# Two-layer graph network on one core: index loads of 64 tiles asked for a body ahead, and four places for the loads of edges

## The reference

```python
h = relu(layernorm(x))                                   # layer 0
m = relu(concat([h[src], edge_attr_64]) @ W_msg.T + b)
m = relu(m @ W_msg2.T + b2)
x = x + concat([h, segment_sum(m, dst) / max(cnt, 1)]) @ W_apply.T + b_apply
h = relu(layernorm(x))                                   # layer 1
alpha = segment_softmax(edge_weight, dst)
agg = normalize(segment_sum(alpha[:, None] * h[src], dst))
comb = normalize(0.5 * (h @ W_self + b_self + agg @ W_nb + b_nb))
x = x + layernorm(comb) * gamma + beta
```

## Time and profile before

| | |
|---|---|
| median of three runs | 10865.57 us |
| the profiled execution | 10872.07 us |
| its span, first to last instruction | 10870.3 us |
| POOL busy | 6155.9 us (57%), 6448 gathers |
| PE busy | 5331.9 us (49%) |
| DVE busy | 3580.0 us (33%) |
| ACT busy | 1136.7 us (10%) |
| DMA engines, mean | 57 GB/s |
| granted TensorE clock, mean | 0.669 of full speed |

### The profile page before, as it was taken

How to read it: one execution, slowest core, us unless ns; L and a number is a source line. 1 busy time by engine, 2 the same in 40 slices (tenths; PEclk the granted TensorE clock), 3 DMA queues, 4 the chain that set the end, 5 groups by cost and what they waited for, 6 DMA issues and landing times.

```text
span 10870.3 us, 94616 instructions
## 1 busy us (share of the span) xinstructions
PE 5331.9 (49%) x26549; PEld 4117.8 (38%) x26549; DVE 3580.0 (33%) x14159; ACT 1136.7 (10%) x2108; POOL 6155.9 (57%) x6486
## 2 busy tenths in 40 slices
PE   4666666666655555566666533332333233233334
PEld 3444444444444344344444423222222222222224
DVE  4333233323222222222222433333333333333336
ACT  2111111111111111111111200000000000000002
POOL 4555555555554444455555466666666666666663
PEclk7777777777777677777777655655555555555556
DMA  4222222222222222222222222221111111111112
GB/s 151 56 57 54 56 56 55 57 58 57 61 67 56 57 57 59 58 55 56 58 56 57 65 57 56 56 55 49 46 46 47 46 46 47 46 46 47 46 47 72
DMA packets 412673, 618.83 MB, mean 57 GB/s; under 512 B 171795, under 2 KB 274175, under 8 KB 411263
## 3 DMA queue, kind: packets, MB, share of 16 engines
q0 software_dynamic: 206336, 422.99, 15.0%
q1 hardware_dynamic: 192624, 183.30, 6.1%
q10 hardware_dynamic: 13200, 6.56, 0.2%
HBM read 576.45 MB, written 35.92 MB: 56 GB/s over the span
## 4 chain that ended last, share of the span: by engine, by line
another core or an unknown queue 49%; PE 25%; issue 12%; DVE 12%; ACT 1%; DVEq 1%; DMA 0%; SPq 0%; POOL 0%; ACTq 0%; POOLq 0%
PE bank L1056 13%; DVE acc L884 7%; PE bank L1118 6%; PE bank L1115 3%; PE bank L1053 2%; DVE onehot L887 1%; DVE work L887 1%; ACT work L581 1%; DVEq L866 1%; DVEq L884 0%; DVE xq L711 0%; DVE acc L711 0%; DVE acc L995 0%; ACT work L587 0%
## 5 line engine op out<-in xcount | busy, mean ns | idle before, releaser
L493 POOL DMA_INDIRECT rows_ring<-p_table,idx x3224 | 3087.5, 958 | 2951.8 <-DMA idx<-in_src_ring 1790.9
L884 DVE TENSOR_TENSOR acc<-acc,bank 128x128 f32 x6448 | 1826.0, 283 | 7192.7 <-remote 5639.5
L493 POOL DMA_INDIRECT rows_ring<-h_table,idx x3224 | 3052.5, 947 | 1635.2 <-issue 1013.2
L887 DVE TENSOR_SCALAR onehot<-iota,dloc,coef 128x128 f32<-128x128 f32 x4840 | 1703.6, 355 | 16.5 <-ACT coef L558 13.3
L1056 PE MATMUL bank<-work,rows_ring 128*128 128x128 f32 x3216 | 694.6, 370 | 1867.6 <-DVE work L887 665.6
L1056 PE MATMUL bank<-onehot,work 128*128 128x128 f32 x6448 | 1094.4, 325 | 863.4 <-issue 676.4
L1056 PE MATMUL bank<-onehot,rows_ring 128*128 128x128 f32 x3232 | 743.8, 401 | 1247.1 <-remote 594.9
L1056 PEld LDWEIGHTS bank<-work,rows_ring 128*128 128x128 f32 x3216 | 597.9, 270 | 1968.7 <-issue 1911.4
L1056 PEld LDWEIGHTS bank<-onehot,work 128*128 128x128 f32 x6448 | 1002.8, 237 | 898.9 <-issue 711.3
L1056 PEld LDWEIGHTS bank<-onehot,rows_ring 128*128 128x128 f32 x3232 | 651.6, 297 | 1323.7 <-issue 1261.4
L1118 PE MATMUL bank<-work,we_sb 64*128 64x512 f32 x1612 | 1045.4, 724 | 164.7 <-issue 164.1
(11 more groups left out here) (121 smaller groups left out, 1066.1 us busy)
## 6 DMA issues: line engine op xcount, KB each, us to landing
work<-in_edge_t SPq DMA_DIRECT2D x403, 256.0 KB
rows_ring<-p_table,idx POOLq DMA_INDIRECT x3224
rows_ring<-h_table,idx POOLq DMA_INDIRECT x3224
idx<-in_src_ring SPq DMA_DIRECT2D x404, 8.0 KB
ht_rows<-rows_ring SPq DMA_DIRECT2D x25, 256.0 KB, 2.3
p_table<-rows_ring SPq DMA_DIRECT2D x25, 256.0 KB, 2.5
work<-ht_rows SPq DMA_DIRECT2D x25, 256.0 KB
h_table<-work ACTq DMA_DIRECT2D x25, 256.0 KB
```

The lines of the kernel that those rows point to most:

```text
L493: pool.indirect_dma_start(out=rows_ring[:, 16 * h + G * k + j, :], out_offset=None, in_=table[:, :], in_offset=bass.IndirectOffsetOnAxis(a ...
L884: dve.tensor_tensor(win, win, ps_sum[layer][k % slots][:, j * P:(j + 1) * P], ALU.add).then_inc(added, 1)
L887: ins = dve.tensor_scalar(hot_slots[layer][k % slots][:, j * P:(j + 1) * P], iota[:, :], dloc[:, ds(t, 1)], coef[:, ds(t, 1)], ALU.is_equa ...
```

## The change

1. `idx` holds the numbers of 2 x 64 tiles' numbers where it held 2 x 16. One load brings the indices of a pair of bodies (32 KB for 8 KB; 51 loads for a layer instead of 202). Pair p + 1 is asked for in body i = 2p (even, from 2), behind that body's edge loads and behind a wait until PE has done the groups before body i (`m1t_in_psum` or `sums1_in_psum` at 8i). It is first used in body i + 2. POOL waits for indices once in two bodies.
2. `ef_ring` has four places: chunks n = 0, 1 (mod 4) on partitions 0 to 63, 2 and 3 on partitions 64 to 127 of the same columns. `we_sb` is loaded twice, once for each half of the partitions. Chunk n waits for chunk n - 4. Each place has its own semaphore.
3. In a body of layer 0 SP issues four edge chunks, then the indices (even bodies), then `load_pre`, which stood between the halves. In layer 1's tail the loads of `self_rows` stand behind the last index loads.

```diff
-        idx = sb("idx", [P, 2, 4 * G], I32)
+        idx = sb("idx", [P, 2, 16 * G], I32)
-        we_sb = sb("we_sb", [DE, P])
+        we_sb = sb("we_sb", [2 * DE, P])
-        ef_ring, m1t_sb, m2_sb = work[0:DE, 0:2048], place[6:8], place[8:10]
+        m1t_sb, m2_sb = place[6:8], place[8:10]
+        ef_ring = [work[DE * (n // 2):DE * (n // 2) + DE, 1024 * (n % 2):1024 * (n % 2) + 1024] for n in range(4)]
...
-            sp.dma_start(we_sb[:, :], we).then_inc(S["weights_loaded"], 16)
+            for n in range(2):
+                sp.dma_start(we_sb[DE * n:DE * n + DE, :], we).then_inc(S["weights_loaded"], 16)
...
-            def load_idx(layer, half, h, turn=None):
-                for k in range(4) if turn is not None else ():
-                    sp.wait_ge(s_rows[layer][4 * h + k], 64 * turn)
-                sp.dma_start(idx[:, h, :], src_ring[ds(half, 1), :, :].rearrange("a p t -> (a p) t")).then_inc(s_idx[layer][h], 16)
+            def load_idx(layer, pair):
+                h = (pair + layer) % 2
+                sp.dma_start(idx[:, h, :], src_ring[pair, :, :]).then_inc(s_idx[layer][h], 16)
...
             def edges0(i, beside=None):
-                for h in range(2):
-                    if h and beside is not None:
-                        load_pre(beside)
-                    half = 2 * i + h
-                    if later(i):
-                        load_idx(0, half, h, i)
-                    for c in range(2):
-                        chunk = 2 * half + c
-                        if isinstance(i, int) and 2 * chunk >= NG:
-                            continue
-                        if later(chunk, 2):
-                            sp.wait_ge(S["m1t_in_psum"], 2 * chunk - 2)
-                        sp.dma_start(ef_ring[:, c * 1024:(c + 1) * 1024],
-                                     edge_t[ds(chunk, 1), :, :].rearrange("a p t -> (a p) t")).then_inc(S2["edges_loaded"][c], 16)
+                for chunk in range(4 * i, min(4 * i + 4, -(-NG // 2))):
+                    if chunk >= 4:
+                        sp.wait_ge(S["m1t_in_psum"], 2 * chunk - 6)
+                    sp.dma_start(ef_ring[chunk % 4], edge_t[chunk, :, :]).then_inc(S2["edges_loaded"][chunk % 4], 16)
+                if i >= 2 and i % 2 == 0 and i // 2 + 1 < NPAIR:
+                    sp.wait_ge(S["m1t_in_psum"], 8 * i)
+                    load_idx(0, i // 2 + 1)
+                if beside is not None:
+                    load_pre(beside)
...
+            def next_idx(i):
+                if i >= 2 and i % 2 == 0 and i // 2 + 1 < NPAIR:
+                    sp.wait_ge(S["sums1_in_psum"], 8 * i)
+                    load_idx(1, i // 2 + 1)
...
             def gather(layer, table, i):
                 used = (S["m1t_in_psum"], S["sums1_in_psum"])[layer]
+                pair = i // 2
+                turn = (pair + layer) % 2
+                if i % 2 == 0:
+                    pool.wait_ge(s_idx[layer][turn], 16 * (pair // 2) + 16)
                 for h in range(2):
-                    pool.wait_ge(s_idx[layer][h], 16 * i + 16)
                     for k in range(4):
                         if later(i):
                             pool.wait_ge(used, 8 * i + 4 * h + k - 7)
```

More of the change, by code:

```diff
@@ L39 @@
 NPOOL = -(-NG // 8)
+NPAIR = -(-NPOOL // 2)
 NTF, NREST = divmod(N, P)
@@ L181, in gnn @@
         S = {n: sem(n) for n in names}
-        pair_names = "ht_stored p_stored h2_stored h2_loaded self_stored edges_loaded idx0_loaded idx1_loaded"
+        pair_names = "ht_stored p_stored h2_stored h2_loaded self_stored idx0_loaded idx1_loaded"
         S2 = {n: [sem(f"{n}_{h}") for h in range(2)] for n in pair_names.split()}
-        S2 |= {n: [sem(f"{n}_{h}") for h in range(4)] for n in ("self_loaded", "out_stored")}
+        S2 |= {n: [sem(f"{n}_{h}") for h in range(4)] for n in ("self_loaded", "out_stored", "edges_loaded")}
         s_x = [sem(f"x_loaded_{n}") for n in range(-(-NBATCH // 3))]
@@ L385, in load_soft @@
                 sp.dma_start(wgt, weight_flat.rearrange("(p l) -> p l", p=P)).then_inc(S["soft_in_loaded"], 16)
-            for h in range(2):
-                load_idx(0, h, h)
+            for pair in range(2):
+                load_idx(0, pair)
             store_scalars(0)
@@ L404, in _ @@
                 loads0(i)
-            sp.wait_ge(S["m1t_in_psum"], NG)
-            for h in range(2):
-                load_idx(1, h, h)
+            assert NPAIR % 2
+            for pair, groups in enumerate((16 * (NPAIR - 1), NG)):
+                sp.wait_ge(S["m1t_in_psum"], groups)
+                load_idx(1, pair)
             for h in range(2):
                 sp.wait_ge(S2["h2_stored"][h], 16 * used(2, h))
+            def next_idx(i):
+                if i >= 2 and i % 2 == 0 and i // 2 + 1 < NPAIR:
+                    sp.wait_ge(S["sums1_in_psum"], 8 * i)
+                    load_idx(1, i // 2 + 1)
             def beside1(c, h, i):
@@ L420, in beside1 @@
                     sp.dma_start(table_rows(self_rows, c - 2), four(self_out[h])).then_inc(S2["self_stored"][h], 16)
-                if later(c):
-                    for half in range(2):
-                        load_idx(1, 2 * c + half, half, c)
+                next_idx(c)
             for c in range(NBATCH + 2):
@@ L447, in _ @@
                 load_self(c)
[L448 to L455, removed]
+            for i in range(NBATCH + 2, NPOOL):
+                next_idx(i)
+            ahead = 14
+            for c in range(4, ahead):
+                load_self(c)
             for c in range(NBATCH):
@@ L487, in gather @@
                             pool.wait_ge(used, 8 * i + 4 * h + k - 7)
-                        if k == 0 or later(i):
+                        if h + k == 0 or later(i):
                             pool.sem_inc(S["pool_turns"], 1)
@@ L494, in gather @@
                                 out=rows_ring[:, 16 * h + G * k + j, :], out_offset=None, in_=table[:, :],
-                                in_offset=bass.IndirectOffsetOnAxis(ap=idx[:, h, G * k + j:G * k + j + 1], axis=0),
+                                in_offset=bass.IndirectOffsetOnAxis(ap=idx[:, turn, 32 * (i % 2) + 16 * h + G * k + j:32 * (i % 2) + 16 * h + G * k + j + 1], axis=0),
                             ).then_inc(s_rows[layer][4 * h + k], 16)
@@ L1072, in _ @@
             pe.wait_ge(S["constants_made"], 7)
-            pe.wait_ge(S["weights_loaded"], 32)
+            pe.wait_ge(S["weights_loaded"], 48)
             pe.wait_ge(S["bias_ready"], 1)
@@ L1109, in layer0 @@
                     if live(i, k, 0):
-                        g, slot, c = 8 * i + k, k % 2, k // 2 % 2
+                        g, slot = 8 * i + k, k % 2
                         pe.wait_ge(s_rows[0][k], 64 * i + 64)
@@ L1115, in layer0 @@
                             pe.matmul(tiles(ps_m1t[slot])[j], rows_ring[:, G * k + j, :], ident[:, :], start=j == 0, stop=False, is_transpose=True)
-                        pe.wait_ge(S2["edges_loaded"][c], 32 * i + 16 * (k // 4) + 16)
-                        at = c * 1024 + slot * 512
-                        pe.matmul(ps_m1t[slot][:, :], we_sb[:, :], ef_ring[:, at:at + 512], start=False, stop=True).then_inc(S["m1t_in_psum"], 1)
+                        chunk, rows_of = k // 2, slice(DE * (k // 4), DE * (k // 4) + DE)
+                        pe.wait_ge(S2["edges_loaded"][chunk], 16 * i + 16)
+                        pe.matmul(ps_m1t[slot][:, :], we_sb[rows_of, :], ef_ring[chunk][:, slot * 512:slot * 512 + 512], start=False, stop=True).then_inc(S["m1t_in_psum"], 1)
                     if live(i, k, 1):
```

2 lines of the change are left out of this document (1 added, 1 removed).

## The result

The changed kernel takes 9887.34 us (median of four runs, 9882.48 to 9889.6), the kernel before 10860.9 us in the same comparison (four runs, 10851.8 to 10873.19). The ratio is 0.9102, 95% interval 0.9087 to 0.9118: the change saves 9%. The forecast was 10070 us, so the gain was larger than forecast by 183 us.

What follows compares the result with a forecast made beforehand. POOL's gathers bound it, resting for indices queued on SP behind edge loads held by PE's late signals. Layer 0's 751 plus layer 1's 42 us off 10872 gave 10079, as a median 10070 us; range 9450 to 10750.

Steps and rivals of the forecast that it cites:

- The bound: Layer 0: POOL waits 1790.9 us for indices queued on SP behind an edge load held by PE's late signal.
- The signs that go with the size of a rest: Layer 0 if right: POOL rests of 4 to 5 us behind runs of 15 to 20 gathers, gathers ending near 5290.
- The pace: Layer 0: 5.0 us of gathers plus a 4.6 us rest per 3.5 groups, 6.31 us a group for 7.09.
- the prompt stretch: Time behind POOL's restart in which PE's signals to other engines still come promptly, taken as 9 us.
- the prediction's own rule: Groups in a cycle: one whose signal was stuck, plus prompt stretch over PE's 3.59 us a group (9 / 3.59 = 2.5).
- The nodes' product: Layer 0's 25 bodies beside it: extra cost falls from 172 us to 50, 2 us a body, between 0 and 172.
- Layer 0's sum: 5086 us for groups, 50 beside the nodes' product, 62 for start and a late load: 5198 us, 751 less.
- Edges: Four edge places: no gain or loss, as PE hardly waits for edges; rows 64 to 127 taken to cost the same.
- Layer 1: Index waits of 84.4 us removed, part returning as rests at full slots: 42 us gained, between 0 and 84.
- Rival A: Only POOL's own gather rate binds layer 0, 4030 us, for some 8870 us in all; chance 5%.
- Rival B: The rest is PE's working time, so slot waits replace index waits at the same length: 10790 to 10870 us; chance 12%.
- rival C: Rests too short to free signals, one group then a rest; slower from a share of 0.34, 11230 us at half; 9%.

Runs made afterwards that it cites:

- rests of fixed length: Changed kernel plus eight chained POOL memsets ahead of every second layer 0 group: 10075.03 us where the kernel before took 10871.89, 9422.66 us where it took 8323.3.
- edges alone: Kernel before with four edge places, indices still by halves in their old place: 10324.86 us (ratio 0.9497); where before took 8323.3 us, 8313.35 (0.9988).
- indices alone: Changed kernel with edges back in two places on partitions 0 to 63: 9879.28 us (ratio 0.909); where before took 8323.3 us, 8312.15 (0.9986).
- run 23: Not a run's label: words of "might itself run 23% faster", said of the unchanged kernel before, which took 8323 us in some sessions and 10861 in others.

## Why the prediction was right, and where it was not

**The bound.** "The rest of 7.55 us is SP's edge load held for PE, with the indices behind it": right. Taken away, the index wait went from 1790.9 us to nothing (forecast under 50). That the slot is late next was right too: 851 us by name (1026 with the rests called "issue" and the four behind DVE) where 900 to 1300 stood. The signs that go with the size of a rest were missed: rests of 4 to 5 us behind runs of 15 to 20 gathers were 2.8 us behind 8 or 12, and layer 0's gathers ended at 5081 us, not near 5290.

**The pace.** Forecast 6.31 us a group, measured 6.14. The time is nearly right, but its two sizes were both off and made up for each other. The rest was put at 4.6 us, by layer 1's rows; 606.5 / 213 is 2.85 (2.8 over the 343 rests counted above). The groups in a cycle were put at 3.5; layer 0 stood 4989 - 4030 = 959 us, which are 959 / 2.85 = 336 rests, or 2.4 groups each (the trace has 347, and 2.3). So 4.6 / 3.5 = 1.31 us a group was 959 / 806 = 1.19. What failed is the step that takes layer 1's rests as the model of a full slot. Why layer 0's are shorter wasn't tried; one reason could be that there the first of three signals frees the slot, where layer 1 has one at the end of a group's work. The 9 us of the prompt stretch were too long as well: at 6 to 9 us behind a restart 88% of the relus are already late, and 45% at 3 to 6 us. With some 6 us for 9 the prediction's own rule gives 6 / 3.59 + 1 = 2.7 groups, an estimate from these shares, near the 2.4. What the rests of fixed length confirm is the direction: with a rest behind each 10 us of gathers few signals are long late, and POOL doesn't wait for PE. That the sum came within 2% of the time is in part luck, since the two sizes erred in opposite directions.

**The nodes' product.** Booked at 2 us a body, 50 us in all. The pace beside it is 6.09 us a group against 6.14, so it is 0: the whole extra cost of 172 us has gone with the index waits behind `load_pre`, of which edges alone shows 25 us a place.

**Layer 0's sum** was 5198 us and is 4989: 806 x 0.17 = 137 us by the pace, 50 us by the product, and 22 of its start and rest.

**Edges.** Booked at nothing: right (9879.28 us without them, 9881 to 9887 with). Rows 64 to 127 cost the same: the products' mean is 726 ns in the changed kernel and 726 in indices alone, where all are on rows 0 to 63.

**Layer 1.** Booked at half of 84 us, 42, and measured 33. **Between the layers** 8 us were lost, which I had at nothing.

**Rival A** (POOL's own rate, 8870 us) did not come in the runs that were predicted. Its premise, that signals are prompt, is what holds in a prompt session, in both layers; there the kernel before already takes 8323 us, and its two parts, run apart, each gain 10 us. The Trainium skill, Advanced Engine Details and Errata, Network/Comms, says a sequencer reads a semaphore in 50 to 100 ns. By that rule the kernel always runs as in a prompt session. The trace agrees with it there (0.04 us), and in a late session it doesn't (8.1 us at 1516.22). **Rival B** (rests of 7 us at slots) and **rival C** (one group, then a rest) did not come. But for the four behind DVE's sums no rest of POOL for a slot in layer 0 is longer than 4.3 us; and of the runs between rests 159 are of three groups, 103 of two and only 45 of one, 6% of the groups, where C needed 34%.

What the prediction missed is its own condition. It reasoned from one profiled execution, and its forecast gain of 7% (measured 9%) is that of a session in which signals come late. It gave no word to the case that the kernel before might itself run 23% faster.

## What to carry to other kernels

A load that the busiest engine waits for should not stand in a queue behind a load that is held for something else; asked for a body or more in advance in the same queue it took away 1791 us of waits, and 960 us of layer 0's time, since new waits came for the rest. When a wait is removed, price the wait that comes next by the rows of the place where it will be, not by the nearest other loop: here 2.85 us for 4.6. And time the parts of a change beside the kernel before in the same session, since a part's worth (9% or 0.1%) can hang on the kind of session in which the base is measured.

## What the runs showed of the hardware

The kernel before takes 10861 to 10872 us in some sessions and 8323 in others, its single runs within 0.4% of each other inside a session, and one chip gave both within a quarter of an hour. Indices alone, of which there is a profile of each kind, takes 4981 and 4635 us for its layers in the one and 4073 and 4026 in the other. In late sessions PE's signals came 8.1 and 14.5 us late at the places shown while POOL issued gathers without a rest; in prompt ones the relu follows by 0.04 us under the same gathers. What sets the kind of session wasn't found: no run here varies anything that could, and it is left open. It is not the granted TensorE clock, which in layer 1 is the higher in the late session (0.58 for 0.50). The late sessions' traces also hold only about a quarter of the semaphore records (34 of 131 thousand for indices alone); whether that goes with the cause or only with the recording isn't known.

Rests of POOL of 2.9 us behind each 10 us of gathers make layer 0 independent of the kind of session (5184 and 5185 us), at their own price, and cut the first relus that start over 5 us late from 244 to 2. That gathers in a long run delay PE's signals to ACT in a late session is thus shown by an edit that touches nothing but POOL; by what path they do so is not.
